# Sending finished expert tiles back in token order, in place of gathering them at the end

## The chip, the cores and the metric

One core of one Trainium2 chip. The time is that of the device for one launch, in microseconds (us); runs of a kernel are given by their median. Engines: PE (TensorE, matrix products), DVE (VectorE), ACT (ScalarE), POOL (GpSimd) and SP (SyncE, which here only issues DMAs). Each runs its own instructions in order; they meet through semaphores.

## The reference, cut to what matters

Two MetaFormer layers on an image tensor x of shape (2, 128, 48, 48), that is 2 images of 2304 tokens with 128 channels. Layer 0 mixes tokens by window attention and has 8 experts, layer 1 mixes them by a convolution block and has 16 gated experts with a hidden size of 256. Each block is added to its input. The last block is the one that the change touches:

```python
probs = softmax(t @ gate_w + gate_b)          # t: normalized tokens, 16 experts
rw, re = top_k(probs, 2)                      # two experts per token
rw = rw / rw.sum(-1)                          # the two gates
y = sum_k rw[:, k] * ((silu(t @ w1[re_k]) * (t @ w2[re_k])) @ w3[re_k])
out = x + t + y
```

All of it is fp32.

## The kernel before

**Layout.** Tokens are kept as 18 tiles of 128 per image (TT = 18): XT is the running sum, TN its normalized form, both in SBUF as [128, 18, 128]. TG = 3 tiles form a group, NG = 6 groups an image. A list `order` names phases; every engine walks it and carries out its part of each phase.

**Routing (phases RC, RP, RS).** DVE picks two experts per token and computes the gates GATE[b]. From prefix sums it derives, for each token and each of its two choices, a slot POS[b][:, k, t] in a list sorted by expert. Each expert's part of the list is padded up to whole tiles of 128, so the list has J = 52 tiles for 36 tiles' worth of choices. Then (L1304 to L1313) it derives which expert each tile belongs to.

**Scatter (phase RS on POOL, L619 to L625).** SP has filled sorted_x in DRAM with zeros from the SBUF tile ZER (L440). POOL issues 36 indirect DMAs per image; each writes the 128 rows of one tile of TN to the slots given by POS. Image 1's batch begins once DVE has written its slots (L1299).

**The expert stage (phase M).** For each image 52 tiles go through four engines as a pipeline. SP loads sorted_x in groups of RING = 4 tiles into one of two buffers XG (L471). PE transposes a tile (L788), ACT copies it out (L984), DVE copies the expert's first weights beside it (L1320), PE multiplies (L797), ACT applies silu (L990), DVE multiplies by the other half (L1328), PE multiplies by w3 (L808), and ACT copies the result to YG (tail, L995). After four tiles SP stores YG to sorted_y in DRAM (L475). PE works on tile j, j - 2 and j - 4 in one step. On DVE, PE, ACT and SP most of this is a loop of two groups a turn.

**Gather and sum (phase F).** When all of image b's tiles are stored, POOL issues 36 indirect DMAs (L627 to L638) that fetch each token's two result rows into G, in token order. G is `gathered_or_att`, of which there is one for both images: image 0's gather runs beside image 1's expert tiles, and image 1's gather waits for out_ready of image 0 group by group. DVE then does XT = XT + G[k] * GATE[k] (L1351), two operations for each tile, and SP stores each group of three tiles to the output (L533). DVE's program has phase F behind both M phases, so image 0's sum too is done after image 1's tiles.

Of the kernel before, what the change touches and what calls it, by code (L numbers as in the profile page):

```python
# [5 lines left out]
def metaformer_program(nc, x_tok, params, consts, pos_bias, out_wT, conv1_wT, conv2_wT, w2_rows, w1_conv,  # L6
                       router_wT, gate_wT, gate_b, moe0_w1, moe0_w2, moe0_b1, moe0_b2, moe1_w12, moe1_w3, out):
# [39 lines left out]
    ROWS = EX[0] * TG  # L47
    C4 = 32
# [6 lines left out]
    with ctx:  # L55
# [11 lines left out]
        xs_dram = [nc.dram_tensor(f"sorted_x{b}", (J * P, P), fp32).ap() for b in range(NB)]  # L67
        ys_dram = [nc.dram_tensor(f"sorted_y{b}", (J * P, P), fp32).ap() for b in range(NB)]
# [5 lines left out]
        TN = [sb(f"normed{b}", [P, TT, P]) for b in range(NB)]  # L74
        QY = [sb(f"qy{b}", [P, NT]) for b in range(NB)]
        big = sb("padded_or_w12", [P, EX[1] * 512 + 4 * RING * P])
# [19 lines left out]
        G = [gath[:, k * TT * P:(k + 1) * TT * P].rearrange("p (t c) -> p t c", c=P) for k in range(2)]  # L96

# [9 lines left out]
        CON = sb("consts", [P, 5 * P + HEADS // 2 + 2 + 32 + 7 * 32 + EMAX + J + TT + RING])  # L107
# [6 lines left out]
        POW = CON[:, o:o + RING]  # L114
        PRM = sb("params", [P, 16])
# [26 lines left out]
        GATE = [sb(f"gate{b}", [P, 2, TT]) for b in range(NB)]  # L142
        o = 0

        def carve(n, width):
# [14 lines left out]
        XG, YG = ([big[:, o + (2 * k + h) * RING * P:o + (2 * k + h + 1) * RING * P].rearrange("p (r c) -> p r c", c=P)  # L160
                   for h in range(2)] for k in range(2))
        XS, YS = ([g[h][:, r, :] for h in range(2) for r in range(RING)] for g in (XG, YG))
        ZER = sb("zeros", [P, 512])
# [164 lines left out]
        def ys_free(eng, b, j, r, h):  # L328

            if r == 0 and (not isinstance(j, int) or b or j // RING >= 2):  # L330
                eng.wait_ge(S(f"ys_out{h}"), (j - RING * h) * (16 // (2 * RING)) + 16 * b * through_buffer(h))

        def gather_part(t):

            return t // TG if t < TT - 1 else NG
# [46 lines left out]
        def _(sp):  # L382
# [20 lines left out]
            def windows_out(b):  # L403

                ln_wait_all(sp, "LNA", b)
                two = grid(b)[0:NW].rearrange("(g two) x n c -> two g x n c", two=2)
                tn = TN[b][:, :, :].rearrange("p (g k) c -> p k g c", k=TG)
# [32 lines left out]
            def zero_fill(b):  # L440
                v = xs_dram[b].rearrange("(n r p) c -> n p r c", p=P, r=RING)
                for n in range(J // RING):
                    sp.dma_start(v[n], ZER[:, :].rearrange("p (r c) -> p r c", c=P)).then_inc(S(f"sorted_zero{b}"), 16)

# [15 lines left out]
            def moe(b):  # L460
                n = J // RING
                ys = ys_dram[b].rearrange("(q r p) c -> q p r c", p=P, r=RING)

                def load(q, h, b=b):

                    xs = xs_dram[b].rearrange("(q r p) c -> q p r c", p=P, r=RING)
                    if not isinstance(q, int) or q >= 2:
                        sp.wait_ge(S("x_transposed"), RING * (q - 1) + b * J)
                    elif b:
                        sp.wait_ge(S("x_transposed"), b * J)  # L470
                    sp.dma_start(XG[h], xs[ds(q, 1)].rearrange("o p r c -> p (o r) c")).then_inc(S(f"xs_in{h}"), 16)  # L471

                def store(q, h):
                    sp.wait_ge(S("y_ready"), RING * (q + 1) + b * J)
                    sp.dma_start(ys[ds(q, 1)].rearrange("o p r c -> p (o r) c"), YG[h]).then_inc(S(f"ys_out{h}"), 16)  # L475

                def load_first(b):
                    sp.wait_ge(S(f"scattered{b}"), 16 * 2 * TT)
                    for q in range(2):
                        load(q, q, b)  # L480

                if b == 0:
                    load_first(0)
                turns = (n - 2) // 2
                with sp.Fori(0, turns) as turn:
                    for h in range(2):
                        load(turn * 2 + (2 + h), h)
                        store(turn * 2 + h, h)
                for q in range(2 * turns, n):
                    if q + 2 < n:  # L490
                        load(q + 2, q % 2)
                    elif q == n - 1 and b == 0:
                        load_first(1)
                    store(q, q % 2)

# [29 lines left out]
            sp.wait_ge(S("zeros_set"), 1)  # L525
            for b in range(NB):
                zero_fill(b)
            moe(0)
            moe(1)
            for b in range(NB):  # L530
                for g in range(NG):
                    sp.wait_ge(S("out_ready"), b * NG + g + 1)
                    sp.dma_start(out[b, :, g * TG:(g + 1) * TG, :], XT[b][:, g * TG:(g + 1) * TG, :]).then_inc(S("out_stored"), 16)  # L533
# [4 lines left out]
        def _(pool):  # L538
            nc.gpsimd.memset(ZER[:, :], 0.0).then_inc(S("zeros_set"), 1)
            nc.gpsimd.memset(HP[0][:, :, :], 0.0).then_inc(S("pad_zero"), 1)  # L540
            nc.gpsimd.memset(PTB, 0.0).then_inc(S("pt_zero"), 1)
            pool.wait_ge(S("consts_in"), 64)

# [75 lines left out]
            def scatter(b):  # L619
                pool.wait_ge(S(f"routed{b}"), 1)  # L620
                pool.wait_ge(S(f"sorted_zero{b}"), 16 * (J // RING))
                for t in range(TT):
                    for k in range(2):
                        nc.gpsimd.indirect_dma_start(xs_dram[b], bass.IndirectOffsetOnAxis(ap=POS[b][:, k, t:t + 1], axis=0),  # L624
                                                     TN[b][:, t, :], None).then_inc(S(f"scattered{b}"), 16)  # L625

            def gather(b):  # L627
                for h in range(2):
                    pool.wait_ge(S(f"ys_out{h}"), 16 * (b + 1) * through_buffer(h))
                if b == 0:  # L630
                    pool.wait_ge(S("gated"), DN)
                for t in range(TT):
                    if b and t % TG == 0:
                        pool.wait_ge(S("out_ready"), t // TG + 1)
                    for k in range(2):
                        nc.gpsimd.indirect_dma_start(G[k][:, t, :], None, ys_dram[b],  # L636
                                                     bass.IndirectOffsetOnAxis(ap=POS[b][:, k, t:t + 1], axis=0)
                                                     ).then_inc(S(f"gathered{gather_part(t)}"), 16)  # L638

            run(A=lambda n: attend(att, n), AN=add_normed, D=dense, XC=pad, RS=scatter, F=gather)  # L640


# [242 lines left out]
        def _(act):  # L885
# [92 lines left out]
            def moe(b):  # L978
# [13 lines left out]
                def tail(j, r, h):  # L992
                    act.wait_ge(S("y_full1"), j + 1 + b * J)
                    ys_free(act, b, j, r, h)
                    nc.scalar.activation(YS[h * RING + r], banks[6 + r % 2][:, 0:P], ACT.Copy).then_inc(S("y_ready"), 1)  # L995

                def step(j, r, h, expert, load):
                    ok = lambda k: not isinstance(j, int) or 0 <= j - k < J
                    if ok(0):
                        xt(j, r)  # L1000
                    if ok(2):
                        nonlin(j - 2, (r + 2) % RING)
                    if ok(4):
                        tail(j - 4, r, 1 - h)

                tile_groups(act, b, step, 4, experts=False)
# [48 lines left out]
            def route_a(l, b, g):  # L1055
# [6 lines left out]
                XG=lambda b, g: evac(QY[b], "XG", b, g), XCE=conv1, GQ=gn_sqrt, XCH=conv_padded, XMH=conv_mid, XU=conv2, XUH=conv_out)  # L1062
# [3 lines left out]
        def _(dve):  # L1066
# [123 lines left out]
            def choose(l, b, piece):  # L1190
# [33 lines left out]
                if piece == 4:  # L1224
# [6 lines left out]
                    tt(GATE[b][:, 0, :], v[0], v[3], ALU.mult)  # L1231
                    ins = tt(GATE[b][:, 1, :], v[1], v[3], ALU.mult)
                    if l == 0:
                        link(ins)
# [80 lines left out]
            def moe(b):  # L1315
# [13 lines left out]

                def step(j, r, h, expert, load):  # L1330
# [3 lines left out]
                    if ok(0):  # L1334
                        weights(j, r, expert(0))
                    if ok(2):
                        first(j - 2, (r + 2) % RING)
# [6 lines left out]
            def combine(b):  # L1344
                for g in range(NG):
                    for part in range(g, g + (2 if g == NG - 1 else 1)):
                        tiles = [t for t in range(g * TG, (g + 1) * TG) if gather_part(t) == part]
                        dve.wait_ge(S(f"gathered{part}"), 16 * 2 * len(tiles) * (b + 1))
                        for k in range(2):
# [121 lines left out]
```

## Time and profile before

| | |
|---|---|
| median of 3 runs | 743.06 us (739.6 to 746.34) |
| span of the profiled execution | 744.4 us |
| PE busy | 562.7 us (76%) |
| DVE busy | 357.5 us (48%) |
| ACT busy | 348.0 us (47%) |
| POOL busy | 389.6 us (52%) |
| mean granted clock of PE | 0.868 |
| DMA | 74.98 MB, mean 101 GB/s |

The profile is one execution. Its span runs from the first to the last instruction. Busy time of POOL includes the making of an indirect DMA's descriptors (the DMA_INDIRECT rows); the data moves after that and is not counted as POOL's time. Matmul ends are modelled, so a busy PE is not PE at its peak.

### The profile page before, as it was taken

How to read it: one execution, taken by the hardware profiler on the slowest of the kernel's cores; microseconds unless marked ns; L12 is line 12 of the kernel's file. 1: busy time of each engine (PE TensorE's matmuls, PEld its weight loads, DVE VectorE, ACT ScalarE, POOL GpSimd, SP SyncE). 2: the span in 40 equal slices, each digit the busy share in tenths (PEclk: the TensorE clock that was granted, in tenths of full speed). 3: DMA queues.
4: the chain of work that ended last, by engine and by line, in shares of the span. 5: the costliest groups of instructions: out<-in, count | busy, mean ns of one | idle time of the engine just before them, and what ended most of it. 6: DMA issues, size and time to landing. Idle time of an engine off the chain costs nothing.

```text
span 744.4 us, 16104 instructions
## 1 busy us (share of the span) xinstructions
PE 562.7 (76%) x5352; PEld 465.2 (62%) x5353; DVE 357.5 (48%) x1036; ACT 348.0 (47%) x843; POOL 389.6 (52%) x445
## 2 busy tenths in 40 slices
PE   0487798879699998999995798453699989999000
PEld 0366677667477776777763575242599989998000
DVE  5877888645401601300127435736555545555521
ACT  1546788975573438622246250340356545555000
POOL 4577899753373986843333000575674017720673
PEclk9999999988897999999985699555699999999555
DMA  9342222211354533331940000112144334541431
GB/s 340 92 125 75 72 77 83 61 50 44 146 203 141 212 136 128 104 110 42 282 128 1 0 1 0 38 52 67 54 139 131 100 92 117 144 117 56 131 85 53
DMA packets 82188, 74.98 MB, mean 101 GB/s; under 512 B 9102, under 2 KB 74854, under 8 KB 81742
## 3 DMA queue, kind: packets, MB, share of 16 engines
q1 hardware_dynamic: 77518, 64.72, 27.3%
q0 software_dynamic: 4608, 9.45, 4.6%
q8 instruction: 37, 0.61, 0.4%
q14 instruction: 25, 0.20, 0.1%
HBM read 50.92 MB, written 23.63 MB: 100 GB/s over the span
## 4 chain that ended last, share of the span: by engine, by line
PE 57%; POOL 12%; DVE 11%; issue 8%; ACT 8%; DMA 3%; SPq 0%; POOLq 0%; DVEq 0%; ACTq 0%
PE bank L797 12%; PE bank L759 8%; PE bank L858 8%; PE bank L742 8%; PE bank L808 6%; POOL gathered_or_att L636 4%; PE bank L311 3%; POOL gathered_or_att L577 3%; PE bank L719 3%; POOL padded_or_w L568 3%; ACT normed L903 2%; DVE ln_stats L1080 2%; POOL gathered_or_att L586 2%; PE bank L788 2%; PE bank L757 1%
## 5 line engine op out<-in xcount | busy, mean ns | idle before, releaser
L612 POOL TENSOR_TENSOR padded_or_w<-padded_or_w,gathered_or_att 128x384 f32<-128x384 f32 x96 | 95.2, 1000 | 87.6 <-ACT padded_or_w L976 72.0
L624 POOL DMA_INDIRECT sorted_x<-normed,slot x72 | 71.4, 992 | 98.5 <-DVE slot L1299 77.2
L636 POOL DMA_INDIRECT gathered_or_att<-sorted_y,slot x72 | 69.5, 966 | 95.4 <-DMA sorted_y<-padded_or_w 74.0
L759 PEld LDWEIGHTS bank<-moe_or_conv,padded_or_w 128*128 128x128 f32 x576 | 82.2, 200 | 32.0 <-issue 10.9
L976 ACT ACTIVATE padded_or_w<-bank,moe_b 128x384 f32<-128x384 f32 x96 | 55.3, 579 | 99.3 <-PE bank L742 99.0
L759 PE MATMUL bank<-moe_or_conv,padded_or_w 128*128 128x128 f32 x576 | 85.5, 287 | 0.0
L742 PE MATMUL bank<-chan_major,moe_or_conv 128*128 128x384 f32 x192 | 81.3, 508 | 0.1
L1328 DVE TENSOR_TENSOR att_or_moe<-att_or_moe,bank 128x256 f32<-128x256 f32 x104 | 43.7, 420 | 57.8 <-PE bank L808 40.6
L990 ACT ACTIVATE att_or_moe<-bank 128x256 f32<-128x256 f32 x104 | 39.9, 383 | 61.7 <-PE bank L797 61.2
L808 PE MATMUL bank<-w,att_or_moe 128*128 x416 | 63.8, 277 | 0.7 <-ACT padded_or_w L995 0.6
L657 PE MATMUL bank<-padded_or_w 64*64 64x64 f32 x1152 | 48.6, 237 | 20.6 <-issue 14.8
L797 PE MATMUL bank<-att_or_moe,chan_major 128*128 128x128 f32 x416 | 56.7, 281 | 7.2 <-DVE chan_major L1320 7.2
L657 PEld LDWEIGHTS bank<-padded_or_w 64*64 64x64 f32 x1152 | 42.5, 149 | 30.0 <-issue 30.0
L1261 DVE TENSOR_TENSOR residual<-residual,bank 128x384 f32<-128x384 f32 x12 | 6.6, 553 | 109.9 <-PE bank L759 109.9
L797 PEld LDWEIGHTS bank<-att_or_moe,chan_major 128*128 128x128 f32 x416 | 52.2, 197 | 7.6 <-issue 7.6
L797 PE MATMUL bank<-chan_major 128*128 128x128 f32 x416 | 55.7, 277 | 0.0
L808 PEld LDWEIGHTS bank<-w,att_or_moe 128*128 128x128 f32 x416 | 54.6, 192 | 1.6 <-issue 1.3
L937 ACT ACTIVATE gathered_or_att<-bank 64x384 f32<-64x384 f32 x96 | 46.2, 481 | 19.5 <-PE bank L668 18.9
L577 POOL TENSOR_TENSOR gathered_or_att<-gathered_or_att,score_max 128x384 f32<-128x384 f32 x48 | 39.8, 829 | 29.5 <-DVE score_max L1155 28.5
L311 PE MATMUL bank<-consts,normed 128*128 128x128 f32 x144 | 29.7, 344 | 33.6 <-DVE normed L1112 23.7
L1320 DVE COPY chan_major<-padded_or_w 128x512 f32 x104 | 44.2, 428 | 20.2 <-PE bank L797 16.7
L797 PEld LDWEIGHTS bank<-chan_major 128*128 128x128 f32 x416 | 51.2, 194 | 0.3
(169 smaller groups left out, 1082.8 us busy)
## 6 DMA issues: line engine op xcount, KB each, us to landing
gathered_or_att<-combine SPq DMA_DIRECT2D x24, 768.0 KB, 4.2
padded_or_w<-windows SPq DMA_DIRECT2D x192, 48.0 KB, 1.9
sorted_x<-zeros SPq DMA_DIRECT2D x26, 256.0 KB, 3.7
padded_or_w<-sorted_x SPq DMA_DIRECT2D x26, 256.0 KB
sorted_y<-padded_or_w SPq DMA_DIRECT2D x26, 256.0 KB, 2.4
padded_or_w<-in_moe_w SPq DMA_DIRECT2D x8, 512.0 KB, 5.3
residual<-in_x_tok SPq DMA_DIRECT2D x2, 1152.0 KB, 6.3
out<-residual SPq DMA_DIRECT2D x12, 192.0 KB, 2.4
```

Source lines behind the costliest of these rows:

```text
L311: ins = nc.tensor.transpose(t_bank(n)[:, k * P:(k + 1) * P], a, IDN)
L577: nc.gpsimd.tensor_tensor(sb_, sb_, MXS[:, hf, :].unsqueeze(2).broadcast_to([P, HW_, KEYS]), ALU.subtract).then_inc(S("shifted"), 1)
L612: nc.gpsimd.tensor_tensor(HB[n % DRING], HB[n % DRING], GB_[k % 3][:, n % 4, :], ALU.mult).then_inc(S("gated"), 1)
L624: nc.gpsimd.indirect_dma_start(xs_dram[b], bass.IndirectOffsetOnAxis(ap=POS[b][:, k, t:t + 1], axis=0), TN[b][:, t, :], None).then_inc(S(f ...
L636: nc.gpsimd.indirect_dma_start(G[k][:, t, :], None, ys_dram[b], bass.IndirectOffsetOnAxis(ap=POS[b][:, k, t:t + 1], axis=0)).then_inc(S(f" ...
L657: ins = nc.tensor.matmul(banks[2 + hf][m, w * KEYS:(w + 1) * KEYS], QBD[n % 4][m, w, :], KG[b][m, row:row + 2, k0:k0 + 2 * Q], start=True, ...
L742: nc.tensor.matmul(banks[HBANK[n % 2]][:, 0:DG], W1E[:, e, :], CM[b][:, g * DG:(g + 1) * DG], start=True, stop=True).then_inc(S("h_full"), 1)
L759: ins = nc.tensor.matmul(acc[:, t * P:(t + 1) * P], HB[n % DRING][:, t * P:(t + 1) * P], W2E[:, e, :], start=False, stop=(e == EX[0] - 1 a ...
L797: ins = nc.tensor.matmul(banks[2 + r % 2][:, a * P:(a + 1) * P], W12S[r][:, a, :], XTS[r][:, :], start=True, stop=True)
L808: ins = nc.tensor.matmul(banks[6 + r % 2][:, 0:P], HID[r][:, a * P:(a + 1) * P], W3[:, ds(e, 1), a, :], start=(a == 0), stop=(a == 1))
L858: ins = nc.tensor.matmul(banks[TAP[b][hh]][:, 0:HALF], TOEP[:, n, :], HP[b][:, hh * NW // 2 + a:hh * NW // 2 + a + NW // 2, kx:kx + IMG], ...
L976: nc.scalar.activation(HB[n % DRING], banks[HBANK[n % 2]][:, 0:DG], ACT.Gelu, bias=B1C[:, e:e + 1]).then_inc(S("gelu"), 1)
```

## The change

**Tokens carry an address and a gate.** A row of sorted_x grows from 128 to 130 words (XR). Word 128 is the row's home, the place in a new DRAM buffer where its result belongs; word 129 is its gate. TN becomes a view of TNR, [128, 18, 130]. POOL writes the homes of first choices into TNR at the start, those of second choices into NEXT; DVE's gates go to the same two tiles. sorted_x is filled no longer with zeros from SBUF but from a DRAM input pad_rows whose rows have homes behind the tokens' rows, so that padding rows land where nobody reads.

**Scatter.** POOL sends the 18 tiles of first choices, then for each half waits until these have landed, copies NEXT into the two last words, and sends the 9 tiles of second choices.

**Expert stage.** DVE copies the two last words of each group of four tiles out of XG (HOMES, as int32, and GSLOT). ACT's tail scales a tile's rows by GSLOT and writes to YR, a ring of 9 groups of 4 tiles in the place of G. POOL, in phase M, sends each finished tile by indirect DMA to `returned`, at the rows in HOMES; SP's stores of YG are gone. ACT's and SP's loops are written out.

**Sum.** When all y_sent of an image have come, SP loads its six groups of 384 KB, plain, 3 KB per partition: image 0's into QY, image 1's into TNR. SP does so for both images behind the last load of sorted_x. DVE adds twice 128x384 per group. The stores to the output are issued by ACT.

The diff, cut to its core:

```diff
-                for t in range(TT):
-                    for k in range(2):
-                        nc.gpsimd.indirect_dma_start(xs_dram[b], ...(ap=POS[b][:, k, t:t + 1], axis=0),
-                                                     TN[b][:, t, :], None).then_inc(S(f"scattered{b}"), 16)
-            def gather(b):
...
+                for t in range(TT):
+                    rows(0, t, f"first_sent{b}{t // half}")
                 for h in range(2):
-                    pool.wait_ge(S(f"ys_out{h}"), 16 * (b + 1) * through_buffer(h))
...
+                    part = slice(h * half, (h + 1) * half)
+                    pool.wait_ge(S(f"first_sent{b}{h}"), 16 * half)
+                    nc.gpsimd.tensor_scalar(TNR[b][:, part, P:XR], NEXT[b][:, part, :], 1.0, None, ALU.mult).then_inc(S("second_tails"), 1)
+                    pool.wait_ge(S("second_tails"), 2 * b + h + 1)
+                    for t in range(h * half, (h + 1) * half):
+                        rows(1, t, f"scattered{b}")
+
+            def send_back(b):
+                for j in range(J):
+                    k = ring_turn(b, j // RING)[1]
+                    if j % RING == 0:
+                        pool.wait_ge(S("tails_read"), b * (J // RING) + j // RING + 1)
+                    pool.wait_ge(S("y_ready"), b * J + j + 1)
+                    nc.gpsimd.indirect_dma_start(yt_dram[b], bass.IndirectOffsetOnAxis(ap=HOMES[b][:, j:j + 1], axis=0),
+                                                 YR[k * RING + j % RING], None).then_inc(S(f"y_sent{k}"), 16)
...
+                def tail(j, r):
+                    turn, k = ring_turn(b, j // RING)
                     act.wait_ge(S("y_full1"), j + 1 + b * J)
-                    nc.scalar.activation(YS[h * RING + r], banks[6 + r % 2][:, 0:P], ACT.Copy).then_inc(S("y_ready"), 1)
+                    if r == 0:
+                        act.wait_ge(S("tails_read"), b * (J // RING) + j // RING + 1)
+                        if turn:
+                            act.wait_ge(S(f"y_sent{k}"), 16 * RING * turn)
+                    nc.scalar.activation(YR[k * RING + r], banks[6 + r % 2][:, 0:P], ACT.Identity, scale=GSLOT[b][:, j:j + 1]).then_inc(S("y_ready"), 1)
...
+                def tails(j, h):
+                    dve.wait_ge(S(f"xs_in{h}"), ...)
+                    nc.vector.tensor_copy(HOMES[b][:, ds(j, RING)], XG[h][:, :, P])
+                    nc.vector.tensor_copy(GSLOT[b][:, ds(j, RING)], XG[h][:, :, P + 1]).then_inc(S("tails_read"), 1)
...
+            def returned_rows(b):
+                y_rows_out(sp, b)
...
+                rows = yt_dram[b][0:2 * NT, :].rearrange("(p g n) c -> g p (n c)", g=NG, n=2 * TG)
+                for g in range(NG):
+                    sp.dma_start(YL[b][g], rows[g]).then_inc(S(f"y_back{b}{g}"), 16)
...
+                    dve.wait_ge(S(f"y_back{b}{g}"), 16)
+                    link(tt(xt, xt, YL[b][g][:, 0:DG], ALU.add))
+                    tt(xt, xt, YL[b][g][:, DG:2 * DG], ALU.add).then_inc(S("out_ready"), 1)
```

POOL's program before, from image 1's scatter to its end (`normed` is TN, `slot` is POS, `gathered_or_att` is G):

```order
L624 DMA sorted_x<-normed,slot 6656x128 [waits sorted_zero1,routed1]
L624 DMA sorted_x<-normed,slot 6656x128 x35
L636 DMA gathered_or_att<-sorted_y,slot 128x128 [waits gated,ys_out1,ys_out0]
L636 DMA gathered_or_att<-sorted_y,slot 128x128 x35
L636 DMA gathered_or_att<-sorted_y,slot 128x128 [waits out_ready,ys_out1,ys_out0]
L636 DMA gathered_or_att<-sorted_y,slot 128x128 x5
L636 DMA gathered_or_att<-sorted_y,slot 128x128 [waits out_ready]
```

And the same stretch after the change; the last two rows come 26 times in all, 13 for each image, and end the program:

```order
L618 DMA sorted_x<-normed,slot 6656x130 [waits homes_set,sorted_zero1,first_gates,routed1]
L618 DMA sorted_x<-normed,slot 6656x130 x17
L626 TENSOR_SCALAR normed<-second_tail 128x9x2 [waits first_sent10]
L618 DMA sorted_x<-normed,slot 6656x130 [waits second_tails]
L618 DMA sorted_x<-normed,slot 6656x130 x8
L626 TENSOR_SCALAR normed<-second_tail 128x9x2 [waits first_sent11]
L618 DMA sorted_x<-normed,slot 6656x130 [waits second_tails]
L618 DMA sorted_x<-normed,slot 6656x130 x8
L637 DMA returned<-gathered_or_att,home_of_slot 11264x128 [waits y_ready,tails_read]
L637 DMA returned<-gathered_or_att,home_of_slot 11264x128 [waits y_ready] x3
```

The gathers are gone; 104 sends stand directly behind image 1's scatter, each behind a wait on its tile.

SP's program before, its end from image 1's last groups on (`padded_or_w` holds XG and YG):

```order
L471 DMA padded_or_w<-sorted_x 128x4x128 [waits x_transposed]
L475 DMA sorted_y<-padded_or_w 128x4x128 [waits y_ready] x3
L533 DMA out<-residual 128x384 [waits out_ready] x12
L55 UNCONDITIONAL_BRANCH [waits out_stored]
```

SP's end after the change, with the loads of image 1's sorted rows in the first two rows:

```order
L475 DMA padded_or_w<-sorted_x 128x4x130 [waits tails_read,x_transposed,scattered1]
L475 DMA padded_or_w<-sorted_x 128x4x130 [waits tails_read,x_transposed] x12
L484 DMA qy<-returned 128x768 [waits y_sent7,y_sent6,y_sent8,y_sent5,t_read0,y_sent4,t_read1,y_sent3,y_sent2,y_sent1,y_sent0]
L484 DMA qy<-returned 128x768 x5
L484 DMA normed<-returned 128x768 [waits y_sent5,y_sent4,y_sent6,y_sent3,y_sent7,y_sent2,y_sent8,y_sent1,y_sent0]
L484 DMA normed<-returned 128x768 x5
L57 UNCONDITIONAL_BRANCH [waits out_stored]
```

The stores have left SP's queue, and twelve plain loads have come to its end, both images' behind the last load of sorted rows.

## Rows read from the trace of the kernel before

**Rows 1.** The page: busy tenths of the span in 40 slices
```profile
PE   0487798879699998999995798453699989999000
POOL 4577899753373986843333000575674017720673
```

**Rows 2.** By stage: length, busy PE PEld DVE ACT POOL, granted clock, DMA share, GB/s
```profile
610.00:656.00 46.00, 45.83 (x401) 45.15 (x402) 23.56 (x61) 25.93 (x93) 34.54 (x36) 1.00 0.49 127
687.00:744.00 57.00, 0.32 (x3) 0.13 (x2) 20.14 (x70) 0.28 (x1) 34.32 (x36) 0.53 0.30 88
```

**Rows 3.** POOL's timeline, both scatters: start, length, line; then L624's landing times
```profile
469.34 1.27 POOL L624 DMA_INDIRECT sorted_x<-normed,slot  x1 [68.92 <-DVE slot L1299]
...
514.91 0.96 POOL L624 DMA_INDIRECT sorted_x<-normed,slot  x1 [0.30 <-issue]
524.10 1.05 POOL L624 DMA_INDIRECT sorted_x<-normed,slot  x1 [8.24 <-DVE slot L1299]
...
569.37 0.96 POOL L624 DMA_INDIRECT sorted_x<-normed,slot  x1 [0.30 <-issue]
...
DMA to landing us min/median/max: 2.2/2.2/3.0
```

**Rows 4.** POOL's timeline, first and last of each gather's 36
```profile
610.79 0.99 POOL L636 DMA_INDIRECT gathered_or_att<-sorted_y,slot  x1 [40.47 <-DMA sorted_y<-padded_or_w]
...
655.70 0.99 POOL L636 DMA_INDIRECT gathered_or_att<-sorted_y,slot  x1 [0.30 <-issue]
690.26 1.03 POOL L636 DMA_INDIRECT gathered_or_att<-sorted_y,slot  x1 [33.57 <-DMA sorted_y<-padded_or_w]
...
734.31 0.94 POOL L636 DMA_INDIRECT gathered_or_att<-sorted_y,slot  x1 [0.30 <-issue]
```

**Rows 5.** Timeline of the end: ACT's last tail, DVE's last sum, the last store
```profile
687.36 0.28 ACT L995 ACTIVATE padded_or_w<-bank 128x128 f32<-128x128 f32 x1 [0.75 <-PE bank L808]
...
736.83 0.74 DVE L1351 SCALAR_TENSOR_TENSOR residual<-gathered_or_att,gate,residual 128x128 f32<-128x128 f32 x2 [1.20 <-DMA gathered_or_att<-sorted_y,slot]
737.60 0.33 SPq L533 DMA_DIRECT2D out<-residual  x1
```

**Rows 6.** L995 by its source line, 530 to 572 us: duration, first and last start
```profile
L995 ACT ACTIVATE padded_or_w<-bank x26: 277/277/278, 534.7 to 571.9; 128x128 f32<-128x128 f32 x26
```

**Rows 7.** DVE's groups by line and shape: count, busy us, mean ns of one
```profile
L1320 DVE COPY chan_major<-padded_or_w 128x512 f32 x104 | 44.2, 428 | 20.2 <-PE bank L797 16.7 <-issue 3.5
L1307 DVE TENSOR_TENSOR expert_cmp<-route_small,consts 128x416 f32<-128x416 f32 x4 | 2.4, 588 | 0.1
L1297 DVE TENSOR_TENSOR route<-route 128x288 f32<-128x288 f32 x4 | 1.8, 458 | 0.1
```

**Rows 8.** Groups by line on ACT and POOL: mean ns, idle before
```profile
L903 ACT ACTIVATE normed<-residual,ln_values 128x128 f32<-128x128 f32 x99 | 40.5, 483 | 4.9 <-DVE ln_values L1103 4.8
L995 ACT ACTIVATE padded_or_w<-bank 128x128 f32<-128x128 f32 x104 | 28.8, 277 | 10.9 <-PE bank L808 4.6
...
L552 POOL TENSOR_SCALAR band_term<-consts,conv_chan 128x32 f32<-128x32 f32 x6 | 2.2, 361 | 0.5
```

**Rows 9.** Timeline of SP and PE at the expert stage's start
```profile
517.16 14.40 SPq L471 DMA_DIRECT2D padded_or_w<-sorted_x  x3
...
519.94 0.45 PE L788 MATMUL bank<-consts,padded_or_w 128*128 128x128 f32 x1 [3.33 <-DMA padded_or_w<-sorted_x]
...
528.71 2.05 PE L797 MATMUL bank<-att_or_moe,chan_major 128*128 128x128 f32 x8 [7.20 <-DVE chan_major L1320]
```

**Rows 10.** By stage, the first input loads: last number is GB/s
```profile
10.00:20.00 10.00, 1.11 (x5) 1.12 (x6) 9.83 (x34) 4.57 (x10) 7.62 (x13) 1.00 0.87 333
```

**Rows 11.** DMA issues: count, KB each, us from issue to landing
```profile
w<-in_moe_w SPq DMA_DIRECT2D x1, 2048.0 KB, 10.3
```

**Rows 12.** POOL's groups by line, in 524 to 570 and 690 to 736 us: mean ns
```profile
L624 POOL DMA_INDIRECT sorted_x<-normed,slot x36 | 35.6, 988 | 18.9 <-issue 10.7 <-DVE slot L1299 8.2
...
L636 POOL DMA_INDIRECT gathered_or_att<-sorted_y,slot x36 | 34.3, 953 | 44.2 <-DMA sorted_y<-padded_or_w 33.6 <-issue 10.7
```

More of the change, by code:

```diff
@@ L64, in metaformer_program @@
         banks = [ctx.enter_context(nc.psum_tensor(f"bank{i}", [P, 512], fp32)) for i in range(8)]
-        xs_dram = [nc.dram_tensor(f"sorted_x{b}", (J * P, P), fp32).ap() for b in range(NB)]
-        ys_dram = [nc.dram_tensor(f"sorted_y{b}", (J * P, P), fp32).ap() for b in range(NB)]
+        xs_dram = [nc.dram_tensor(f"sorted_x{b}", (J * P, XR), fp32).ap() for b in range(NB)]
+        yt_dram = [nc.dram_tensor(f"returned{b}", (2 * NT + J * P, P), fp32).ap() for b in range(NB)]
         xv_dram = [nc.dram_tensor(f"windows{b}", (GRID * GROW, P), fp32).ap() for b in range(NB)]
@@ L95, in metaformer_program @@
         gath = sb("gathered_or_att", [P, 2 * TT * P])
-        G = [gath[:, k * TT * P:(k + 1) * TT * P].rearrange("p (t c) -> p t c", c=P) for k in range(2)]
+        YR = [gath[:, k * P:(k + 1) * P] for k in range(YRING * RING)]
         GB_ = [gath[:, k * 4 * DG:(k + 1) * 4 * DG].rearrange("p (e n) -> p e n", n=DG) for k in range(3)]
@@ L142, in metaformer_program @@
         GATE = [sb(f"gate{b}", [P, 2, TT]) for b in range(NB)]
+        NEXT = [sb(f"second_tail{b}", [P, TT, 2]) for b in range(NB)]
+        HOMES = [sb(f"home_of_slot{b}", [P, J], i32) for b in range(NB)]
+        GSLOT = [sb(f"gate_of_slot{b}", [P, J]) for b in range(NB)]
         o = 0
@@ L159, in metaformer_program @@
         HB = [big[:, o + k * DG:o + (k + 1) * DG] for k in range(DRING)]
[L160 to L163, printed above, removed]
+        XG = [big[:, o + h * RING * XR:o + (h + 1) * RING * XR].rearrange("p (r c) -> p r c", c=XR) for h in range(2)]
+        XS = [XG[h][:, r, 0:P] for h in range(2) for r in range(RING)]
+        YL = [[a[:, k * 6 * P:(k + 1) * 6 * P] for a in pair for k in range(NG // 2)]
+              for pair in (QY, [t[:, :, :].rearrange("p t c -> p (t c)") for t in TNR])]
         GST = sb("gn_stats", [P, 6, 6])
@@ L326, in through_buffer, with ring_turn, y_rows_out @@
             return (J // RING + 1 - h) // 2
[L328 to L335, printed above, removed]
+        def ring_turn(b, q):
+            return divmod(b * (J // RING) + q, YRING)
+        def y_rows_out(eng, b):
+            last = b * (J // RING) + J // RING - 1
+            for k in range(YRING):
+                eng.wait_ge(S(f"y_sent{k}"), 16 * RING * ((last - k) // YRING + 1))
         def run(**phases):
@@ L458, in gates @@
                 sp.dma_start(GB_[k % 3].rearrange("p e n -> p (e n)"), rows.unsqueeze(0).broadcast_to([P, 4 * DG])).then_inc(S(f"gates{k % 3}"), 16)
[L460 to L494, printed above, removed]
@@ new lines, in sorted_rows @@
+            def sorted_rows(b, q):
+                xs = xs_dram[b].rearrange("(q r p) c -> q p r c", p=P, r=RING)
+                if q == 0:
+                    sp.wait_ge(S(f"scattered{b}"), 16 * TT)
+                if q >= 2 or b:
+                    sp.wait_ge(S("x_transposed"), RING * max(q - 1, 0) + b * J)
+                    sp.wait_ge(S("tails_read"), max(q - 1, 0) + b * (J // RING))
+                sp.dma_start(XG[q % 2], xs[q]).then_inc(S(f"xs_in{q % 2}"), 16)
+            def returned_rows(b):
+                y_rows_out(sp, b)
+                for k in range(NB if b == 0 else 0):
+                    t_wait_all_read(sp, "XZ", k)
+                rows = yt_dram[b][0:2 * NT, :].rearrange("(p g n) c -> g p (n c)", g=NG, n=2 * TG)
+                for g in range(NG):
+                    sp.dma_start(YL[b][g], rows[g]).then_inc(S(f"y_back{b}{g}"), 16)
@@ L524, in _ @@
                     combine_rows(1)
-            sp.wait_ge(S("zeros_set"), 1)
             for b in range(NB):
                 zero_fill(b)
[L528 to L533, printed above, removed]
+            for q in range(J // RING):
+                sorted_rows(0, q)
+            for q in range(J // RING):
+                sorted_rows(1, q)
+            returned_rows(0)
+            returned_rows(1)
             sp.wait_ge(S("out_stored"), 16 * NB * NG)
@@ L542, in _ @@
             pool.wait_ge(S("consts_in"), 64)
+            for b in range(NB):
+                nc.gpsimd.tensor_scalar(TNR[b][:, :, P], HOME, 1.0, None, ALU.mult).then_inc(S("homes_set"), 1)
+                nc.gpsimd.tensor_scalar(NEXT[b][:, :, 0], HOME, float(TG), None, ALU.add).then_inc(S("homes_set"), 1)
             pool.wait_ge(S("small_in"), 16 * 7)
@@ L643, in _ @@
+            run(A=lambda n: attend(att, n), AN=add_normed, D=dense, XC=pad, RS=scatter, M=send_back)
         @block.tensor
@@ L990, in nonlin, with store @@
                     nc.scalar.activation(SG[r % 2][:, :], banks[2 + r % 2][:, 0:256], ACT.Silu).then_inc(S("silu"), 1)
-                def tail(j, r, h):
+                def tail(j, r):
+                    turn, k = ring_turn(b, j // RING)
                     act.wait_ge(S("y_full1"), j + 1 + b * J)
-                    ys_free(act, b, j, r, h)
-                    nc.scalar.activation(YS[h * RING + r], banks[6 + r % 2][:, 0:P], ACT.Copy).then_inc(S("y_ready"), 1)
[L997 to L1006, printed above, removed]
+                    if r == 0:
[3 more added lines that the diff above has]
+                    nc.scalar.activation(YR[k * RING + r], banks[6 + r % 2][:, 0:P], ACT.Identity, scale=GSLOT[b][:, j:j + 1]).then_inc(S("y_ready"), 1)
+                if b == 0:
+                    act.wait_ge(S("gated"), DN)
+                for j in range(J + 4):
+                    if j < J:
+                        xt(j, j % RING)
+                    if 0 <= j - 2 < J:
+                        nonlin(j - 2, (j - 2) % RING)
+                    if j >= 4:
+                        tail(j - 4, j % RING)
+            def store(b):
+                for g in range(NG):
+                    act.wait_ge(S("out_ready"), b * NG + g + 1)
+                    nc.scalar.dma_start(out[b, :, g * TG:(g + 1) * TG, :], XT[b][:, g * TG:(g + 1) * TG, :]).then_inc(S("out_stored"), 16)
             def gn_sqrt(name, b):
@@ L1230, in choose @@
                     link(nc.vector.reciprocal(v[3], v[2]))
[L1231 to L1232 removed]
                     if l == 0:
[L1234 removed]
+                        tt(GATE[b][:, 0, :], v[0], v[3], ALU.mult)
+                        link(tt(GATE[b][:, 1, :], v[1], v[3], ALU.mult))
+                    else:
+                        dve.wait_ge(S("homes_set"), 2 * NB)
+                        tt(TNR[b][:, :, P + 1], v[0], v[3], ALU.mult)
+                        tt(NEXT[b][:, :, 1], v[1], v[3], ALU.mult).then_inc(S("first_gates"), 1)
                 if piece == 5 and l == 0:
@@ L1345, in combine @@
                 for g in range(NG):
[L1346 to L1349, printed above, removed]
-                            for t in tiles:
-                                ins = nc.vector.scalar_tensor_tensor(XT[b][:, t, :], G[k][:, t, :], GATE[b][:, k, t:t + 1], XT[b][:, t, :], ALU.mult, ALU.add)
-                            if k == 0:
-                                link(ins)
-                    ins.then_inc(S("out_ready"), 1)
+                    xt = XT[b][:, g * TG:(g + 1) * TG, :].rearrange("p t c -> p (t c)")
+                    dve.wait_ge(S(f"y_back{b}{g}"), 16)
+                    link(tt(xt, xt, YL[b][g][:, 0:DG], ALU.add))
+                    tt(xt, xt, YL[b][g][:, DG:2 * DG], ALU.add).then_inc(S("out_ready"), 1)
             def gn(ph, chunks, gamma, beta):
@@ L1449 @@
         b2_rows[:, t, t] = a["L0_ffn_b2"]
+    pad_rows = np.zeros((52 * P, P + 2), np.float32)
+    pad_rows[:, P] = 2 * 18 * P + np.arange(52 * P)
     bc = lambda v: np.broadcast_to(v, (P,) + v.shape)
```

45 lines of the change are left out of this document (24 added, 21 removed).

## The prediction

> **What bounds the kernel now.** I read the page's slices first [rows 1]. From the thirtieth slice (about 540 us) PE is at 9 tenths almost throughout, the second expert layer; in the last three slices PE is at 0 while POOL still works. The table by stage [rows 2] puts numbers on it: from 610 to 656 us PE is busy 45.8 of 46 us at a granted clock of 1.00, the higher level of 2.4 GHz; from 687 on it does nothing and POOL is busy 34.3 of 57 us. So the end of the kernel is first PE's, then POOL's.
>
> What POOL does there is in its timeline. A token row is moved by an indirect DMA of 128 rows. There are four batches of 36: scatter of image 0, scatter of image 1 [rows 3], gather of image 0 under image 1's expert work, and gather of image 1 after everything [rows 4]. The reader is to see two things. First, POOL issues one every 1.25 to 1.3 us, 0.95 to 1.05 busy and 0.30 "issue", and nothing else holds it up. Second, the last batch lies bare: 690.26 to 735.25, some 45 us, and it waits for the store of the last sorted outputs. Behind it stand one landing, two adds and a store [rows 5], then the end at 744.4.
>
> The expert tiles themselves come off PE at a steady pace: 26 tail copies (L995) from 534.7 to 571.9 are one per 1.49 us [rows 6], and the last of the 104 starts at 687.36 [rows 5], so (687.36 - 534.7)/103 = 1.482 us each.
>
> **What the change removes.** Both gathers: 72 indirect DMAs. Only image 1's 36 are bare. Also 26 stores to sorted_y and 72 small DVE multiply-adds.
>
> **What it adds, and where.** 104 indirect sends (all 52 tiles of each image, padding tiles too), on the same in-order POOL queue, behind scatter(1). PE's tile takes 1.48 us and a send about 1.29, so at first look the sends hide wholly. They don't: POOL is late when they begin. Scatter(1) occupies POOL from 524.10 on, and by then the tiles are piling up. The end is therefore set by POOL, and its chain is the sum:
>
> - Scatter(1) starts at 524.10, released by the DVE cast L1299 as before. 36 issues at (569.37 - 524.10)/35 = 1.293 us give 46.5 [rows 3]. Its two waits on first_sent cost nothing: nine issues (11.6 us) lie between the DMA waited for and the wait, against 2.2 to 3.0 us to land [rows 3]. The two tail copies on POOL are like L552 (361 ns, [rows 8]) with 0.30 of issue each, not below nothing and 1.3 us together at most; I take 1.2. POOL reaches the first send at 571.8.
> - By then 26 tiles are ready [rows 6], and 36 fit in the ring. The ring doesn't fill: tile 36 is written at 534.7 + 36 x 1.482 = 588, and the first four sends have landed at 571.8 + 3.9 + 2.2 = 578. From there POOL gains 0.19 us a tile, too little to catch 26 tiles up before PE ends: at 687.4 it has started (687.4 - 571.8)/1.288 = 90 of 104. Neither y_ready nor tails_read ever holds POOL.
> - 103 steps to the start of the last send. Beside expert work the two batches shown ran at 1.293 and (655.70 - 610.79)/35 = 1.283, mean 1.288; on an idle core at (734.31 - 690.26)/35 = 1.259 [rows 4]. 89 x 1.288 + 14 x 1.259 = 132.2, so 704.0. The semaphore wait on each send is new; gather(1) waits on out_ready at every sixth and its steps there are not longer, so I price it at nothing. Low end 103 x 1.259 = 129.7; high end 103 x 1.302 = 134.1, the pace of scatter(0), (514.91 - 469.34)/35 [rows 3].
> - Landing 2.2 from the start of the issue, 706.2. SP reacts at once: the last of scatter(0) started at 514.91, the load behind it at 517.16 [rows 3, 9].
> - Six loads of 384 KB, 2.36 MB. The trace has no such load alone. A 256 KB load took from 517.16 to 519.94, 2.8 us [rows 9], of which 0.8 is transfer at 333 GB/s [rows 10], so 2.0 fixed. Plus 7.1 us at 333 GB/s [rows 10]: 9.1, the low end. The slowest comparable is one 2048 KB load that took 10.3 among others [rows 11], 11.6 scaled to 2304 KB, the high end. At the end nothing else loads, which is nearer the first; I take 9.7: 715.9.
> - Two dependent DVE adds of 128x384 for the last group. From 458 ns at 288 and 588 at 416 columns [rows 7], 0.555 each, 1.15 with the link: 717.05.
> - Store and end: the last DVE operation before ended at 737.57 and the span at 744.4 [rows 5], 6.8 us. Issuing from ACT instead of SP changes little. 723.85.
>
> Against the span of 744.4 this is 20.5 us less. That span is 1.3 us above the median of the runs, 743.06, so the time is 743.06 - 20.5 = 722.5 us. In short, ending = 591.65 + 103p, p being POOL's step; it reaches the old 744.4 at p = 1.483.
>
> **What is free, and under what cover.** Image 0's six loads wait behind image 1's last x load on SP (some ten tiles before the end, 687.4 - 14.8, near 672) and are in SBUF before DVE leaves the expert stage near 687; its twelve adds, 7 us, and its stores lie under POOL's remaining sends (to 704). Uncovered they would cost 7 us. On DVE each group of four tiles gets two copies of 128x4 (0.07 to 0.2 us each) and a wait; DVE is busy 23.6 of 46 us [rows 2], PE gets its hidden tiles two steps later, and PE's own pace has some 17 us to spare against POOL. ACT's tail copy gets a scale per partition: L903, with scale and bias, takes 483 ns at the same size, L995 277 [rows 8]. At worst ACT's 25.9 us busy of 46 [rows 2] grow by 31 x 0.2 = 6.4. SP no longer stores, and the x loads come no later. Scatter(0) gets the same two copies; its end moves from 516 to about 517, the x load to 519, landed near 522, while PE waits for a DVE copy until 528.71 anyway [rows 9]: 6 us of cover. The fill of sorted_x from a DRAM tensor, some 7 MB, stands where the zeros' stores stood on SP, and POOL idles 68.92 us before image 0's scatter, whose releaser is DVE [rows 3]. Four small POOL operations come at the start, 1.4 us at L552's price, where POOL is busy 4 tenths [rows 1]. Uncovered they would cost those 1.4 us.
>
> **A rule that speaks against it.** DVE copies 128x512 words per tile in 428 ns, quicker per column than an addition of 416 columns in 588 [rows 7]; POOL makes its descriptors beside 104 of them. The rows show what that costs: an issue lasts 988 ns beside these copies and routing, 953 without [rows 12], 0.035 us. It is in the 1.288. The Trainium skill, "SBUF — State Buffer", section "SBUF: two separate sides", says that such a copy locks GpSimd out of the shared port, that a DMA from GpSimd which takes 620 ns alone takes 3100 overlapped. By that factor of five, as an estimate, the 104 sends alone would take 104 x (5 x 0.96 + 0.30) = 530 us. The trace disagrees so far, with 72 issues.
>
> **Rivals.**
> - *An issue is held for a whole copy* (the other side: slower). If each indirect DMA in the stage met one DVE copy in full, the step would be 1.259 + 0.43 = 1.69: scatter(1) ends 14 us later (585.8), the last send starts at 759.9, the end is 779.8, a time near 778. It decides from p = 1.483 on (1.555 for 1% slower). For it: every send now has such a copy near it. Against it: [rows 12]. 5%. The Trainium skill page cited above names the mechanism; the price here is from rows.
> - *A scattered row of 520 bytes costs two pieces instead of one* (130 words in place of 128), slower: the issue is 1.92 and the step 2.22. Scatter(0) ends at 550.5, the first tiles come 27 us later, scatter(1) ends at 631.9, the sends begin there: 631.9 + 132.7 + 19.85 = 784, a time near 783. The trace shows only 128-word rows, so nothing excludes it; the 0.95 us looks like a price per row. 5%.
> - *PE's pace becomes the bound* through the longer ACT and DVE work or late x loads of 520-byte rows. It decides above (704 - 534.7)/103 = 1.64 us a tile. At 1.68 (the 0.2 us of L903 laid bare on every tile) the last tile is at 707.9 and the end at about 728, time 727. 10%.
> - *The indirect send is slower into DRAM at scattered rows or with a wait on each*, p about 1.43 without either cause above: end 591.65 + 147.3 = 739, time 738, within 1%. Scatters, which also write DRAM rows, took 1.26 to 1.30. 6%.
> - The forecast as summed: 74%.
>
> **How the numbers follow.** The known ends of the forecast's terms are -2.5 and +1.9 (sends), -0.6 and +1.9 (loads), about 1 for the rest, and the runs of before spread by 3.3 us about the median: 716 to 729. PE's pace lies inside; toward the slower sends the range reaches 733. Low 716, high 733. About 1% is what a measurement of this kernel tells from no change. Faster by over 1% (under 735.6): 74 + 10 and part of the slower send, 0.84. Within 1%: 0.06. Slower: 0.10.
>
> **What would show it.** In the changed kernel's trace: POOL's first send near 572 and a step of 1.29 with "issue" ahead of it and no ACT releaser; the last send starting near 704, over 15 us after the last tail on ACT; the six last loads landed within 10 us of it; DVE's last add near 717. Wrong would be: sends released by ACT tail rows (PE is the bound), issues of 1.4 us or more, POOL reaching the first send after 575, or a last load 12 us or more behind.

## The result and the profile after

The changed kernel takes 720.83 us (median of 4 runs, 718.24 to 722.22); the one before, in the same comparison, 742.87 us. The ratio is 0.9666 with a 95% interval of 0.9633 to 0.9699: 3.3% faster. The forecast was 722.5, range 716 to 733. The profiled execution spans 720.4 us, 24.0 less than the 744.4 of before. The medians differ by 22.0; the execution profiled before was one of the slower runs.

The page's slices, as in [rows 1], of the changed kernel:

```profile
PE   0477889679699999999996689736169999999900
POOL 5587799864085686663342100077477777777771
```

POOL has no gap left from the thirtieth slice to the last but one: it works 7 tenths throughout, beside PE and then behind it. PE is idle in two slices at the end instead of three.

The sum's first terms stand in POOL's timeline (start, length, line, and in brackets the idle time before with its releaser). These are the start of image 1's scatter, one of the two tail copies, the first send, and the last:

```profile
523.19 1.06 POOL L618 DMA_INDIRECT sorted_x<-normed,slot  x1 [7.72 <-DVE slot L1310]
...
546.15 0.33 POOL L626 TENSOR_SCALAR normed<-second_tail 128x18 f32<-128x18 f32 x1
546.77 1.03 POOL L618 DMA_INDIRECT sorted_x<-normed,slot  x1 [0.28 <-POOL normed L626]
...
570.90 0.95 POOL L637 DMA_INDIRECT returned<-gathered_or_att,home_of_slot  x1 [0.30 <-issue]
...
704.61 0.95 POOL L637 DMA_INDIRECT returned<-gathered_or_att,home_of_slot  x1 [0.30 <-issue]
```

They answer to [rows 3, 4]. The last send starts 29.7 us earlier than the last gather did (734.31), though POOL now issues 104 sends in place of 72 gathers. Of these 29.7 us, 5.7 are given back behind it: from the start of POOL's last issue to the end it was 10.1 us before and is 15.8 now, since six loads stand there. ACT's last tail and DVE's and SP's last work, to be read beside [rows 5]:

```profile
683.05 0.37 ACT L999 ACTIVATE gathered_or_att<-bank,gate_of_slot 128x128 f32<-128x128 f32 x1 [0.73 <-PE bank L808]
...
706.99 2.69 SPq L484 DMA_DIRECT2D normed<-returned  x6
...
710.14 0.56 DVE L1367 TENSOR_TENSOR residual<-residual,normed 128x384 f32<-128x384 f32 x1 [21.81 <-DMA normed<-returned]
...
717.50 0.56 DVE L1368 TENSOR_TENSOR residual<-residual,normed 128x384 f32<-128x384 f32 x1
```

The last tile is ready at 683.4 and its send starts at 704.6: 21 us of backlog on POOL, where the sum had 17.

### The profile page after: what moved, and what is told of

It is laid out like the page before. It is cut to its first block, busy times and chain, and to the rows that moved or that the text cites. A ratio compares the mean times of both kernels' runs of the same rounds, so it can differ in the third digit from the quotient of the medians.

```text
span 720.4 us, 15997 instructions
## 1 busy us (share of the span) xinstructions
PE 557.8 (77%) x5352; PEld 462.0 (64%) x5353; DVE 356.0 (49%) x1040; ACT 355.9 (49%) x843; POOL 424.4 (59%) x484
## 4 chain that ended last, share of the span: by engine, by line
PE 59%; DVE 12%; POOL 10%; ACT 8%; issue 7%; DMA 3%; SPq 1%; POOLq 0%; DVEq 0%; ACTq 0%
PE bank L797 13%; PE bank L759 9%; PE bank L858 8%; PE bank L742 8%; PE bank L808 7%; POOL gathered_or_att L567 3%; PE bank L719 3%; POOL padded_or_w L558 3%; PE bank L317 3%; ACT normed L903 2%; POOL returned L637 2%; DVE ln_stats L1088 2%; POOL gathered_or_att L576 2%; PE bank L788 2%; PE bank L757 1%
## 5 line engine op out<-in xcount | busy, mean ns | idle before, releaser
L637 POOL DMA_INDIRECT returned<-gathered_or_att,home_of_slot x104 | 103.3, 993 | 31.7 <-issue 22.3
L657 PE MATMUL bank<-padded_or_w 64*64 64x64 f32 x1152 | 46.8, 231 | 21.2 <-issue 15.5
L657 PEld LDWEIGHTS bank<-padded_or_w 64*64 64x64 f32 x1152 | 40.8, 143 | 30.4 <-issue 30.4
L1331 DVE COPY chan_major<-padded_or_w 128x512 f32 x104 | 45.9, 445 | 19.6 <-PE bank L797 17.2
```

The lines of the kernel that those rows point to most:

```text
L637: nc.gpsimd.indirect_dma_start(yt_dram[b], bass.IndirectOffsetOnAxis(ap=HOMES[b][:, j:j + 1], axis=0), YR[k * RING + j % RING], None).then ...
L657: ins = nc.tensor.matmul(banks[2 + hf][m, w * KEYS:(w + 1) * KEYS], QBD[n % 4][m, w, :], KG[b][m, row:row + 2, k0:k0 + 2 * Q], start=True, ...
```

## The experiments

### The changed kernel again, and with fewer sends

This input's routing fills 44 of the 52 tiles of each image. Four kernels ran beside each other. The first is the changed kernel as it is.

> The changed kernel once more, as the yardstick for the runs beside it. Both theories: a span near 720.4 us, POOL's last send starting near 704.6, first send near 570.9, the step between sends 1.298 us.

The second and third leave sends of empty tiles out; what waits for them counts accordingly:

```diff
+        SENT = (44, 52)                       # the third kernel: (44, 44)
             def send_back(b):
-                for j in range(J):
+                for j in range(SENT[b]):
```

> The changed kernel without the sends of image 0's tiles 44 to 51. This input's routing fills 44 of 52 tiles, so these eight hold only padding rows; the kernel leaves them unsent and nothing else. Theory 1 (POOL's queue of indirect DMAs sets the end): the last send starts 8 x 1.298 = 10.4 us earlier, near 694.2, and the span is 710.0. Theory 2 (PE's expert tiles, or loads and stores around them, set the end and POOL only trails them): the last tile is still ready at 683, at most 1 or 2 us change in the span.

> The same with image 1's tiles 44 to 51 unsent too, 88 sends in all. Theory 1: the last send starts 16 x 1.298 = 20.8 us earlier, near 683.8, span 699.6; image 1's last filled tile is ready near 671.7, so POOL still sets the end. Theory 2: as in the run with eight, no more than the 11.6 us by which the last needed tile is earlier.

The fourth does this for any routing. DVE writes the count of filled tiles; POOL reads it:

```diff
+                used[b] = pool.value_load(USED[b][0:1, 0:1], min_val=2 * TT, max_val=J)
+                for q in range(YRING):
+                    group(q, f"y_sent{ring_turn(b, q)[1]}")
+                for i, (first, last) in enumerate(pieces):   # tiles 36 to 43, 44 to 51
+                    with pool.If(used[b] > first * RING):
+                        for q in range(first, last):
+                            group(q, f"rest{b}{i}")
```

The optional tiles have semaphores of their own. POOL later waits for those it has sent and raises rest_sent by one, for which ACT and SP wait.

> The whole computation for any routing: DVE writes the number of filled tiles, POOL reads it and branches around tiles 36 to 43 and 44 to 51 of each image, 8 branches in all. Theory 1: as with 88 sends, plus at most 0.3 us for each branch and 1 us for the last wait on POOL: span 700 to 703. Theory 2: no gain over the changed kernel. A third possibility: the branches keep POOL's sequencer from running ahead and each costs some us, span 705 to 712.

| | median us | ratio to before (95%) | first send | last send | span |
|---|---|---|---|---|---|
| as changed | 722.59 | 0.9686 (0.964 to 0.9732) | 571.27 | 704.97 | 720.6 |
| 8 unsent | 710.61 | 0.9524 (0.9475 to 0.9573) | 569.45 | 693.05 | 709.2 |
| 16 unsent | 703.74 | 0.941 (0.9347 to 0.9472) | 573.72 | 686.38 | 702.8 |
| branches | 700.53 | 0.9394 (0.9358 to 0.9431) | 573.55 | 686.18 | 702.7 |

Theory 1 holds. Each row must be read from its own first send, since the profiled executions differ by up to 4 us in what comes before it: 103 steps take 133.70 us in the first, 95 take 123.60 in the second, 87 take 112.66 in the third, that is 1.298, 1.301 and 1.295 us a step. Eight sends less are 10.1 us, sixteen 21.0. The span of the third came out 3.2 us above what was expected, and 2.8 of that lie ahead of the first send (573.72 against 570.9); the fourth's lies at the upper end of its range, with its first send as late. Theory 2 would have left the second kernel where the first was; it is 11.4 us shorter.

The branches cost nothing that these runs show: 87 steps in 112.63 us against 112.66. So the third possibility is out. The fourth kernel is 22 us under the changed kernel in the same comparison (722.59 to 700.53) and level with the third: their intervals overlap. Its last two sends, in POOL's timeline:

```profile
684.92 0.96 POOL L651 DMA_INDIRECT returned<-gathered_or_att,home_of_slot  x1 [0.30 <-ACT gathered_or_att L1028]
686.18 1.27 POOL L651 DMA_INDIRECT returned<-gathered_or_att,home_of_slot  x1 [0.30 <-ACT gathered_or_att L1028]
```

and in ACT's timeline the tail of image 1's last filled tile, the ninth from the end, and the very last tail, of an empty tile:

```profile
675.64 0.37 ACT L1028 ACTIVATE gathered_or_att<-bank,gate_of_slot 128x128 f32<-128x128 f32 x1
...
685.66 0.37 ACT L1028 ACTIVATE gathered_or_att<-bank,gate_of_slot 128x128 f32<-128x128 f32 x1 [0.74 <-PE bank L835]
```

The last filled tile is ready at 676.0 and its send starts at 686.18, so POOL still runs 10 us late: its queue sets the end here too.

### What the bare gather cost

In the kernel before:

```diff
                     if b and t % TG == 0:
                         pool.wait_ge(S("out_ready"), t // TG + 1)
+                    if b and t < TT - TG:
+                        continue
```

> The kernel before with 30 of image 1's 36 gathers left out (the first five groups of its sum use rows that image 0's gathers left). Theory (the gather lay bare at the end, 1.25 us each): the last six are issued when image 0's sum is done, from about 696.7 to 703.9, instead of 735.25, so 31 us less on POOL. The span by theory A of the drain is 703.9 + 9 = 713, by theory B (the store alone) 709.5.

One profiled run. The span is 711.2 us, 33.2 less than before; the last gather starts at 703.62 instead of 734.31, 30.7 us less. So the gather's issues did lie bare. The stretch doesn't close wholly, since another wait takes part of their place: the first of the six gathers starts at 697.20, behind image 0's sum on DVE ("40.54 <-DVE residual L1353"), which was hidden under the gather before. The span lies between what theory A (713) and theory B (709.5) had. The 2.5 us beyond the issues belong to the end: POOL's closing instruction ended at 711.05 and SP's at 709.0, as the next experiment explains.

### The end: the last store or POOL's drain

The term "store and end" of the sum, 6.8 us, measured 2.3: 718.06 to 720.4. So something else stood at the end before. On each engine the program's closing line (L55 before, L57 after) has an instruction that the profile calls DRAIN. The source-line view gives count, duration in ns and start; of before, two rows:

```profile
L55 POOLq DRAIN  x1: 23858/23858/23858, 720.3 to 720.3; - x1
...
L55 SPq DRAIN  x1: 7/7/7, 739.7 to 739.7; - x1
```

POOL's ends at 720.3 + 23.9 = 744.2, SP's at 739.7: SP had seen the last store land by then, and the span ended at 744.4, with POOL. The same view of the changed kernel:

```profile
L57 POOLq DRAIN  x1: 23695/23695/23695, 690.4 to 690.4; - x1
...
L57 SPq DRAIN  x1: 7/7/7, 720.2 to 720.2; - x1
```

POOL's ends at 714.1, under the loads and adds. To test whether it can set the end, 12 indirect DMAs were put at the end of POOL's program in the changed kernel:

```diff
+            for t in range(12):
+                nc.gpsimd.indirect_dma_start(extra_dram, bass.IndirectOffsetOnAxis(ap=POS[0][:, 0, t:t + 1], axis=0),
+                                             YR[4 * RING + t % RING], None).then_inc(S("extra_sent"), 16)
```

> The changed kernel with 12 more indirect DMAs at the end of POOL's program, into a DRAM tensor that nobody reads or waits for. POOL's last issue moves from 705.6 to about 720.7. Theory A (when all else is done, the end waits for POOL's drain, which ends 8.7 us after POOL's last issue): the drain ends near 729.4 and the span is 729.6, 9.2 us longer, though the last add and store don't move. Theory B (the end waits for the last store alone): the span stays within 1 us of 720.4.

Its median is 726.18 us, ratio to before 0.9731 (0.966 to 0.9803), and its span 723.4. The interval overlaps the changed kernel's (0.964 to 0.9732), so the times alone don't show that it is slower; the rows of its trace do. First the last extra issue in POOL's timeline, then the rows of its closing line:

```profile
718.57 0.96 POOL L643 DMA_INDIRECT extra_rows<-gathered_or_att,slot  x1 [0.30 <-issue]
```

```profile
L57 POOLq DRAIN  x1: 19110/19110/19110, 704.1 to 704.1; - x1
...
L57 SPq DRAIN  x1: 7/7/7, 719.3 to 719.3; - x1
```

SP is done at 719.3, POOL's drain ends at 704.1 + 19.1 = 723.2, and the span at 723.4. So an end set by POOL's drain is real (theory A), and theory B, the store alone, is off by 4 us in this trace. Its size was wrong (729.6 expected): the drain ended 3.7 us behind the last issue's end, not near 8.7. In the kernel with 30 gathers left out it is 6.5 (704.57 to 711.05, the span ending at 711.2), before 9.0, in the changed kernel 8.5. What sets its length stays open.

### DVE's copy beside POOL's issue

```diff
+                    n = 512 if isinstance(j, int) and not b and j < RING else 8
-                    nc.vector.tensor_copy(W12S[r]..., W12[:, ds(e, 1), :]...)
+                    nc.vector.tensor_copy(W12S[r]...[:, 0:n], W12[:, ds(e, 1), 0:n]...)
```

> The changed kernel with DVE's weight copy of 128x512 words cut to 128x8 from the fifth tile on (the experts' first weights are then wrong for these tiles; everything else runs as it did). By the rows: the step between sends falls from 1.298 to 1.26 us, the last send starts 3 to 4 us earlier, span 716 to 717. By a lock that holds an issue for a whole copy, the step would already be 1.69 with the copies; if a smaller part of it acts, the step falls to 1.26 all the same and the copies' share is the difference. If the step stays 1.298, what slows POOL is something else (the other DVE operations, or DMA traffic).

The first send starts at 570.21, the last at 701.13: 1.271 us a step against 1.298. The median is 719.17, the span 716.4 with 720.6 in the yardstick's run (from the other comparison; the kernel before took 745.79 us in that one and 746.07 in this). POOL's group of sends between 600 and 682 us, first of the changed kernel (count, busy, mean ns of one, idle):

```profile
L637 POOL DMA_INDIRECT returned<-gathered_or_att,home_of_slot x64 | 63.4, 991 | 19.5 <-issue 12.8 <-ACT gathered_or_att L999 6.4 <-DVE gate_of_slot L1345 0.3
```

then with the short copy:

```profile
L637 POOL DMA_INDIRECT returned<-gathered_or_att,home_of_slot x66 | 63.2, 958 | 20.1 <-issue 14.6 <-ACT gathered_or_att L999 4.9 <-DVE gate_of_slot L1346 0.6
```

991 against 958 ns: the copies cost an issue 0.033 us. The 0.035 read from [rows 12] is that size, but it compares scatters with gathers, and a gather's issue is some 14 ns shorter by itself (medians of 944 and 958 ns in the trace of before), so the agreement is in part luck.

The step was expected to fall to 1.26 and falls to 1.271. Where the rest sits can be read from POOL's timeline of the changed kernel, behind PE's last tiles:

```profile
683.57 1.27 POOL L637 DMA_INDIRECT returned<-gathered_or_att,home_of_slot  x1 [0.30 <-ACT gathered_or_att L999]
685.14 1.23 POOL L637 DMA_INDIRECT returned<-gathered_or_att,home_of_slot  x1 [0.30 <-issue]
...
687.94 1.22 POOL L637 DMA_INDIRECT returned<-gathered_or_att,home_of_slot  x1 [0.30 <-issue]
689.47 0.95 POOL L637 DMA_INDIRECT returned<-gathered_or_att,home_of_slot  x1 [0.30 <-issue]
```

Up to 683.57 a step is 1.295 us, the next four are 1.475 each, and from 689.47 on it is 1.262. With the short copy the first of these falls to 1.262, which is 0.033 again; the four slow steps stay (683.82 to 689.77). They stand beside DVE's adds of image 0 (681.8 to 688.3) and its stores; no run tells which of these slows them.

The Trainium skill's factor of five for a DMA issued beside such a copy ("SBUF — State Buffer", "SBUF: two separate sides") isn't seen here: the sends' issues last 954 to 1266 ns in the changed kernel, and the view of their line has 2.2 to 3.9 us from issue to landing.

### ACT's loop written out, in the kernel before

```diff
-                tile_groups(act, b, step, 4, experts=False)
+                for j in range(J + 4):
+                    step(j, j % RING, (j // RING) % 2, None, None)
```

> The kernel before with ACT's loop over expert tiles written out, nothing else. In the changed kernel the tails of 104 tiles span 149.3 us, before 152.6, though single tiles take 1.45 in both; the rest are stalls of 0.2 to 1 us at five places and 1.8 us at the change of image. If ACT's loop makes the stalls, the stage shrinks by 1.5 to 3.3 us and the span to 741 to 743; if the stores in SP's queue or the loads behind them make them, nothing changes.

One profiled run: the tails span from 534.0 to 686.5, 152.5 us, and the span is 743.7. ACT's loop is not what made the changed kernel's stage 3.3 us shorter. Whether the stores in SP's queue were, wasn't tried; in the changed kernel those 3.3 us are off the path.

## Why the prediction was right, step by step

| step | predicted | measured |
|---|---|---|
| scatter(1) starts | 524.10 | 523.19 |
| from there to the first send | 47.7 | 47.7 |
| 103 steps to the last send | 132.2 | 133.7 |
| landing, to SP's first load | 2.2 | 2.4 |
| six loads and the last adds | 10.85 | 11.07 |
| from the last add to the end | 6.8 | 2.3 |
| end | 723.85 | 720.4 |

**POOL's queue is the bound.** Right, and shown by leaving sends out. The prediction's sign "no ACT releaser" didn't come out to the letter: 30 of the 104 sends name ACT's tail. But the idle time before any send is 0.30 or 0.31 us, named or not, which is POOL's own gap and no wait.

**The two batches' pace as a price for the sends.** 1.288 beside expert work and 1.259 alone were predicted; overall it was 1.298, so the sum had 1.5 us too little. Some 0.6 of it are the 87 steps beside expert work at 1.295, and 0.9 the four slow steps beside image 0's adds and stores, which the sum counted as alone. The wait on each send cost nothing to be seen.

**The cover.** Image 0's loads, adds and stores lay where they were put, but for the loads, which began at 667.5 (near 672 in the prediction): the adds from 681.8 to 688.3, well under POOL's sends, though not quite free, if the four slow steps are theirs. The two small DVE copies for four tiles took 177 and 171 ns and ACT's scaled tail 368 in place of 277 ns, less than L903's 483. A tile still took 1.45 us in the steady stretch, as before; the prediction's 1.482 is the average with the stalls in it. The tail copies on POOL (L626) took 0.29 to 0.33 us and 0.28 of gap behind them, a little under the 0.36 and 0.30 priced.

**Store and end.** Here the sum went wrong by 4.5 us. The step reads "the last DVE operation before ended at 737.57 and the span at 744.4, 6.8 us", and takes this for the store's. Only 2.1 us of it are (SP was done at 739.7; in the changed kernel it is 2.3 to the very end). The other 4.7 us were POOL's drain, which belongs to the bare gather and leaves the path with it. The sum named the right length and the wrong owner. It was partly offset: the other terms were 1.0 us short in all, so the gain in span was 24.0 us where the sum had 20.5. That the median came out only 1.7 us under the forecast is in part luck. The prediction names 1.3 us between its span, 744.4, and the median, 743.06, but these are a span and a device time. The changed kernel's profiled run took 722.22 us for a span of 720.4, and by these 1.8 us the run profiled before took about 746.2 (an estimate), 3 us over its median; the changed kernel's was 1.4 over its own. So the medians lie 2 us closer together than the spans, and hide that much of the sum's error.

**The rivals.** A send held for a whole copy (p = 1.69): measured 1.298. Rows of 520 bytes at two pieces a row: 36 scatter issues and two tail copies took 47.7 us, as priced from rows of 512 bytes, so nothing of it. PE's pace as the bound: the last tile was ready 21 us before its send. A slower send, 1.43: no.

## What to carry to other kernels

Where an engine's in-order queue of small DMAs is to hide under other work, count all of the queue from the moment it can start, not the rate alone: 1.29 us beside 1.45 us looked hidden and wasn't, because the queue began 26 tiles late. Padding that is free on one engine is paid for on another: in the changed kernel PE had time to spare for the 16 empty tiles, POOL paid 21 us for sending them, and with this input's routing a branch round the sends was worth as much as the change itself. Before reading the stretch from the last work to the end as one term, look at each engine's closing instructions; a drain there can belong to work that the change removes.

## What was not expected of the hardware

POOL's closing drain ended 3.7 to 9.0 us after the end of its last indirect DMA's issue, in executions that end with indirect DMAs, and it is on the path when nothing longer follows (744.2 of 744.4 before, 723.2 of 723.4 with the extra DMAs). With the branches, where POOL first waited until its last sends had landed, the drain started at 689.4 and still took 8.7 us (698.1), so it isn't the landing of the sends that it waits for:

```profile
L57 POOLq DRAIN  x1: 8732/8732/8732, 689.4 to 689.4; - x1
```
